# A graph-attention and mean-aggregation kernel: a new setup order, an earlier score store and other first banks

## Chip, cores and metric

The kernel runs on one core of a Trainium2 chip (trn2). The metric is the device time of one execution in microseconds. The time before is the median of three runs, 3327.2 us.

## What is computed

Two layers for 16 graphs of 1024 nodes with 512 features. The first is attention over neighbours with 8 heads of 64 units; the second averages the neighbours' rows, joins them to the own row and multiplies by a weight. Each has a relu, a residual and a layer norm.

```python
feats   = einsum('bnf,hfu->bhnu', x, W)
e_self  = einsum('bhnu,hu->bhn', feats, a_self)
e_neigh = einsum('bhnu,hu->bhn', feats, a_neigh)
dense   = leaky_relu(e_self[..., :, None] + e_neigh[..., None, :], 0.2)
dense   = dense + NEG_BIG * (1.0 - A[:, None])
gat     = relu(concat_heads(einsum('bhij,bhju->bhiu', softmax(dense), feats) + b))
x1      = layernorm(x + gat)
agg     = einsum('bij,bjf->bif', adj, x1) / max(sum(adj, -1), 1e-6)
out     = layernorm(x1 + relu(einsum('bnf,of->bno', concat(x1, agg), W1)))
```

## The kernel before

The program is written by hand for five engines, each with its own list of instructions, joined by semaphores. SyncE issues all DMAs, in the order in which they are written. One graph is one batch. 1024 nodes are T = 8 row tiles of 128, and 512 features are KC = 4 chunks. TensorE has 8 banks of PSUM.

**A batch** (`batch` in each engine's list) has these stages. The features are products of transposed rows with layer one's weights, each operand split in a high and a low part, so one feature tile is 12 matmuls of 512 columns (`features`, `split_product`, recorded at line 889 as all matmuls are). The scores of all 16 score rows come from 12 matmuls for each half of the nodes (`scores`) with weights that were multiplied by the attention vectors beforehand. ScalarE copies each half into sc_row (`score_rows`, line 486). SyncE stores the row to memory (`store_scores`, line 345) and loads each head's row back, broadcast over the partitions, into s_bc (`load_scores`, line 350). In the heads, ScalarE makes a step word for each of 64 pairs of head and key tile (`make_step`, line 497) from s_bc, VectorE shifts it by the adjacency into a mask word (`mask_word`, line 727), and TensorE multiplies 8 query tiles by 3 parts and 2 kinds for each (`key_tile`, 48 matmuls of 65 columns). VectorE also makes the values of each head (`value_parts`, lines 631 to 637) and adds up the sums (`head_sums`, lines 653 and 655). After the heads come the layer norm (VectorE, ScalarE and GpSimd), the aggregation with the transposed adjacency (`aggregate`, 128x512 matmuls), and layer two (`own`, `neighbours`).

**Overlap of batches.** The rows of the next batch are transposed (`turn_x`, line 918), copied (`x_high`, line 462) and split (`x_low`, line 664) inside the batch; its first half of scores and its feature tiles 0 to 3 stand between the heads and the aggregation. Feature tiles 0 and 1 are computed into banks 0 and 1, tiles 2 and 3 into banks 4 and 5; VectorE empties them with the bias (`feature_rows`, line 669). The aggregation uses the banks AGG_BANKS, (0, 1, 2, 6) for the first half and (7, 3, 0, 1) for the second, and TensorE waits for ft_sb 2 of the next batch before its first matmul, which goes to bank 0.

**Around a batch's end.** SyncE transposes the adjacency words of the next batch (`turn_adj`, line 327), stores output tiles (`store_y`, line 340), and ends the batch with the store of tile 7. Then `first_scores` stores the second score half of the next batch, waits until both halves have landed, and loads the rows of heads 0 and 1. y_out and the slots 2 and 3 of the mask words are the same memory; VectorE waits for the y stores before it makes the values of head 0 (lines 709 and 710), and for the transposes before mask word 0.

**The setup, before batch 0.** SyncE loads layer one's weights, the first four row tiles, the attention vectors, the bias, layer two's weights (2 MB, into the memory xs of the layer's input), row tiles 4 to 7 and adjacency tiles 2 and 3. It then waits for all of layer two's transposes, loads the eight x tiles into xs, and the other adjacency tiles. VectorE splits layer one's weights (lines 600 and 602), makes the attention weights in 16 passes of 512 elements (lines 608 and 610) and splits them. TensorE waits for layer two's weights, turns them in eight groups through banks 0 and 1 (line 898), ScalarE copying (line 467) and VectorE splitting (line 620), and then for the attention weights. Only then come row tiles 0 to 3, `scores(0, 0)`, four feature tiles and row tiles 4 to 7. ScalarE makes the eight adjacency words (`adj_words`, line 480) last, and each word from the fourth on waits for a transpose to free one of three slots.

Of the kernel before, what the change touches and what calls it, by code (L numbers as in the profile page):

```python
# [15 lines left out]
P = 128  # L16
# [27 lines left out]
def gat_sage_kernel(nc, x, adj, gat_w, gat_b, gat_self, gat_neigh, sage_w, out):  # L44
# [22 lines left out]

    XT_BANKS = (6, 7, 6, 7, 0, 1, 0, 1)
# [6 lines left out]
    with ExitStack() as ctx:  # L75
# [106 lines left out]
        def adj_rows_at(t):  # L182
# [5 lines left out]
        w_raw = feat[:, 0:4, :, :].rearrange("p a b c -> p (a b c)")[:, 0:KC * HU].rearrange(  # L188
            "p (c n) -> p c n", c=KC)
        a_bc = z  # L190
        prod = y_out
# [106 lines left out]
        def _(sp):  # L298
            for c in range(KC):
                sp.dma_start(w_raw[:, c, :].rearrange("p (h u) -> p h u", h=H),  # L300
                             gat_w[:, col(c), :].rearrange("h p u -> p h u")).then_inc(w_in[0], 16)
            for t in range(HALF):
                sp.dma_start(lead_x[:, t, :], x[0, t * P:(t + 1) * P, :]).then_inc(lead_in[t].sem, 16)
# [3 lines left out]
            sp.dma_start(sage_raw, sage_w.rearrange("(c p) f -> p c f", p=P)).then_inc(w_in[3], 16)  # L307
# [5 lines left out]

            def load_lead(b, t):
                sp.dma_start(lead_x[:, t, :], x[b, t * P:(t + 1) * P, :]).then_inc(lead_in[t].sem, 16)
# [36 lines left out]
            def first_scores(b):  # L352

                store_scores(b, 1)
                sp.wait_ge(s_stored.sem, s_stored.at(b, 32))
                load_scores(b, 0)
                load_scores(b, 1)
# [5 lines left out]
            sp.wait_ge(w1_ps, 2 * KC)  # L363
            for t in range(T):
                load_x(0, t)
# [3 lines left out]
            store_scores(0, 0)  # L369
            for t in range(T):  # L370
                turn_adj(0, t)
                if t + 4 < T:
                    load_adj(0, t + 4)
            for b in range(B - 1):
                first_scores(b)
                for s in range(2):
                    sp.wait_ge(deg_row.sem, deg_row.at(b, 5 + s))
                    load_lead(b + 1, 2 * s)
                    load_lead(b + 1, 2 * s + 1)
# [30 lines left out]
                store_y(b, T - 1)  # L410
# [49 lines left out]
        def _(act):  # L460
# [4 lines left out]
            for c in range(2 * KC):  # L465
                act.wait_ge(w1_ps, c + 1)
                copy(w1h[:, c, :], bank[c % 2][:]).then_inc(w1_hi, 1)
# [117 lines left out]
            for t in range(HALF):  # L585
                x_high(0, t)
            score_rows(0, 0)
# [3 lines left out]
            for t in range(T):  # L591
                adj_words(0, t)
# [4 lines left out]
        def _(dve):  # L597
# [5 lines left out]
            dve.wait_ge(w_in[1], 32)  # L603
            dve.wait_ge(consts, N_CONST)
            n = 0
            for c in range(KC):
                for k in range(2):
                    dve.tensor_tensor(prod[:, 0], w_raw[:, c, :], a_bc[:, k, :], ALU.mult).then_inc(wa_step, 1)
                    dve.wait_ge(wa_step, n + 1)
                    dve.tensor_reduce(wa32[:, c, k * H:(k + 1) * H], prod[:, 0].rearrange("p (h u) -> p h u", h=H),  # L610
                                      AX.X, ALU.add).then_inc(wa_step, 1)
                    dve.wait_ge(wa_step, n + 2)
                    n += 2
            dve.tensor_copy(wah, wa32[:]).then_inc(w_ready, 1)
            dve.wait_ge(w_ready, 3)
            dve.tensor_tensor(wal, wa32[:], wah.bitcast(F32),
                              ALU.subtract).then_inc(w_ready, 1)
            for c in range(2 * KC):
                dve.wait_ge(w1_hi, c + 1)
                dve.tensor_tensor(w1l[:, c, :], bank[c % 2][:], w1h[:, c, :].bitcast(F32),  # L620
                                  ALU.subtract).then_inc(w1_lo, 1)
# [57 lines left out]
            def batch(b, more):  # L679
# [29 lines left out]
                for s in range(2):  # L709
                    dve.wait_ge(y_stored[s], b * (16 * T // 2) + 16)  # L710
# [22 lines left out]
                feature_rows(b, 7)  # L733
                mask_word(2)
# [138 lines left out]

            dve.wait_ge(w_in[2], 16)
            ones_column(0)
            for t in range(HALF):
                x_low(0, t)
            for t in range(HALF):
                feature_rows(0, t)
            first_maximum(0)  # L880
            for t in range(HALF, T):
                x_low(0, t)
            for b in range(B):
# [3 lines left out]
        def _(pe):  # L887
# [4 lines left out]
            pe.wait_ge(consts, 1)  # L892
            pe.wait_ge(w_in[3], 16)
            for f in range(2 * KC):
                if f >= 2:
                    pe.wait_ge(w1_lo, f - 1)
                for c in range(KC):
                    ins = pe.transpose(bank[f % 2][:, col(c)], sage_raw[:, c, f * P:(f + 1) * P], ident[:])
                ins.then_inc(w1_ps, 1)
            pe.wait_ge(w1_lo, 2 * KC)  # L900
            pe.wait_ge(w_ready, 4)
            pe.wait_ge(consts, N_CONST)
# [37 lines left out]
            def batch(b, more):  # L940
# [60 lines left out]
                if more:  # L1001
# [7 lines left out]
                    pe.wait_ge(ft_sb.sem, ft_sb.at(b + 1, 2))  # L1009
# [34 lines left out]
                def aggregate_first(jt, part):  # L1044
                    part_ok = (x1_hi, x1_lo)[part]
                    pe.wait_ge(part_ok.sem, part_ok.at(b, jt + 1))
                    for f in range(KC):
# [26 lines left out]

            for t in range(HALF):
                turn_x(0, t)
            scores(0, 0)
            for t in range(HALF):
                features(0, t)
            pe.wait_ge(ft_sb.sem, ft_sb.at(0, 2))  # L1080
            for t in range(HALF, T):
                turn_x(0, t)
            for b in range(B):
# [23 lines left out]
```

## Time and profile before

| | us |
|---|---|
| runs (three), median | 3327.2 (3321.91 to 3328.36) |
| profiled execution, its own time | 3327.12 |
| span of its one core | 3325.3 |
| TensorE busy | 3233.3 |
| VectorE busy | 2353.1 |
| ScalarE busy | 1866.8 |
| GpSimd busy | 283.5 |

The profile is one execution. The span is divided among the engines as busy time, and idle time before an instruction is put down to whatever released it. The ends of matmuls are modelled, so the pitch from one start to the next tells their real cost. In a timeline a bracket shows the idle time before a row and its releaser.

### The profile page before, as it was taken

How to read it: one execution, taken by the hardware profiler on the slowest of the kernel's cores; microseconds unless marked ns; L12 is line 12 of the kernel's file. 1: busy time of each engine (PE TensorE's matmuls, PEld its weight loads, DVE VectorE, ACT ScalarE, POOL GpSimd, SP SyncE). 2: the span in 40 equal slices, each digit the busy share in tenths (PEclk: the TensorE clock that was granted, in tenths of full speed). 3: DMA queues.
4: the chain of work that ended last, by engine and by line, in shares of the span. 5: the costliest groups of instructions: out<-in, count | busy, mean ns of one | idle time of the engine just before them, and what ended most of it. 6: DMA issues, size and time to landing. Idle time of an engine off the chain costs nothing.

```text
span 3325.3 us, 124497 instructions
## 1 busy us (share of the span) xinstructions
PE 3233.3 (97%) x56896; PEld 2747.0 (83%) x56896; DVE 2353.1 (71%) x4236; ACT 1866.8 (56%) x2456; POOL 283.5 (9%) x251
## 2 busy tenths in 40 slices
PE   4999999999999999999999999999999999999998
PEld 3978879788796978969789697897978879697895
DVE  3857858587685867858678585785858758587685
ACT  2746647365564655646466474664746647465563
POOL 0020100202002020010200102010020200202001
PEclk8999999999999999999999999999999999999999
DMA  6235251341514315252162422525135151441501
GB/s 180 73 64 149 62 138 55 92 128 57 143 61 105 108 50 151 67 111 89 50 157 67 113 88 59 150 64 131 64 79 140 57 143 50 105 119 51 135 32 51
DMA packets 368653, 314.48 MB, mean 95 GB/s; under 512 B 285056, under 2 KB 285056, under 8 KB 368128
## 3 DMA queue, kind: packets, MB, share of 16 engines
q1 hardware_dynamic: 368128, 306.52, 34.1%
q8 instruction: 446, 7.31, 0.9%
q14 instruction: 79, 0.65, 0.1%
HBM read 205.26 MB, written 34.08 MB: 72 GB/s over the span
## 4 chain that ended last, share of the span: by engine, by line
PE 84%; DVE 7%; DMA 5%; ACT 2%; issue 1%; SPq 0%; DVEq 0%; POOL 0%; ACTq 0%
PE six L889 73%; PE pair L889 10%; DVE mask L727 2%; DMA s_bc<-self_scores 2%; DMA out_dram<-mask 1%; DMA self_scores<-sc_row 1%; PE pair L918 1%; DVE rest L635 1%; PE six L918 1%; DVE x_parts L631 1%; ACT trh L462 1%; DVE feat L669 1%; ACT step L497 1%; DMA adj_t<-adj_word 0%; DVE trl L664 0%
## 5 line engine op out<-in xcount | busy, mean ns | idle before, releaser
L889 PE MATMUL six<-x_parts,mask 128*128 128x65 bf16 x16384 | 1547.9, 192 | 21.1 <-DVE mask L727 21.1
L889 PEld LDWEIGHTS six<-x_parts,mask 128*128 128x128 fp8e4 x16384 | 1536.8, 97 | 30.2 <-issue 20.5
L889 PE MATMUL six<-third,mask 128*128 128x65 bf16 x16384 | 1547.7, 192 | 1.9 <-issue 1.6
L889 PE MATMUL six<-rest,mask 128*128 128x65 bf16 x16384 | 1548.0, 195 | 1.3 <-issue 1.2
L889 PEld LDWEIGHTS six<-third,mask 128*128 128x128 fp8e4 x16384 | 1537.0, 98 | 2.5 <-issue 2.4
L889 PEld LDWEIGHTS six<-rest,mask 128*128 128x128 fp8e4 x16384 | 1531.7, 96 | 1.7 <-issue 0.8
L497 ACT ACTIVATE step<-s_bc,n_step 128x1024 uint16<-128x1024 f32 x1024 | 1089.1, 1137 | 378.3 <-DVE mask L727 344.7
L727 DVE TENSOR_TENSOR mask<-adj_t,step 128x1024 uint16<-128x1024 uint16 x1024 | 649.9, 685 | 60.5 <-ACT step L497 60.5
L889 PE MATMUL six<-adj_t,x_parts 128*128 128x512 fp8e4 x1536 | 385.2, 379 | 16.2 <-DVE trl L857 5.4
L440 POOL TENSOR_TENSOR s_bc<-feat,rden 128x512 f32<-128x512 f32 x112 | 124.6, 1118 | 2789.9 <-DVE s_bc L770 2776.2
L889 PEld LDWEIGHTS six<-adj_t,x_parts 128*128 128x128 f16 x1536 | 144.8, 98 | 206.1 <-issue 19.6
L462 ACT ACTIVATE mask<-six,rdeg 128x512 f32<-128x512 f32 x128 | 87.9, 687 | 234.8 <-PE six L889 234.8
L653 DVE TENSOR_TENSOR x_parts<-six,qry_w 128x130 f32<-128x130 f32 (+2 forms) x272 | 110.6, 407 | 145.4 <-PE six L889 145.1
L889 PE MATMUL six<-w1h,trh 128*128 128x512 f32 x512 | 210.0, 410 | 0.0
L462 ACT ACTIVATE trh<-six 128x512 fp32r<-128x512 f32 x160 | 87.9, 598 | 203.3 <-PE six L889 171.3
L889 PE MATMUL six<-w1l,trh 128*128 128x512 f32 x512 | 199.7, 390 | 0.0
L889 PE MATMUL six<-w1h,trl 128*128 128x512 f32 x512 | 199.7, 390 | 0.0
L857 DVE TENSOR_TENSOR trl<-six,trh 128x512 fp32r<-128x512 f32 x96 | 60.2, 683 | 186.1 <-ACT trh L462 186.1
L520 ACT ACTIVATE x_parts<-xs,nb,rs 128x512 f16<-128x512 f32 x128 | 104.2, 814 | 141.4 <-DVE nb L791 141.4
L889 PE MATMUL six<-w0h,trh 128*128 128x512 f32 x448 | 177.1, 395 | 0.0
L889 PE MATMUL six<-w0l,trh 128*128 128x512 f32 x448 | 177.1, 395 | 0.0
L446 POOL TENSOR_TENSOR x_parts<-xs,x_parts 128x512 f16<-128x512 f32 x128 | 160.8, 1256 | 190.5 <-ACT xs L523 190.5
(125 smaller groups left out, 4566.9 us busy)
## 6 DMA issues: line engine op xcount, KB each, us to landing
s_bc<-self_scores SPq DMA_DIRECT2D x128, 512.0 KB, 3.8
mask<-in_adj_dram SPq DMA_DIRECT2D x64, 512.0 KB, 4.5
xs<-in_x_dram SPq DMA_DIRECT2D x128, 256.0 KB, 4.2
adj_nat<-in_adj_dram SPq DMA_DIRECT2D x64, 512.0 KB, 4.3
out_dram<-mask SPq DMA_DIRECT2D x128, 256.0 KB, 3.5
adj_nat<-in_x_dram SPq DMA_DIRECT2D x64, 256.0 KB, 5.8
step<-in_x_dram SPq DMA_DIRECT2D x64, 256.0 KB, 3.9
xs<-in_L_gnn_W_dram SPq DMA_DIRECT2D x1, 2048.0 KB, 12.3
```

The costliest lines, as they stand in the source:

```text
L440: pool.tensor_tensor(z[:, t % 2].rearrange("p (h u) -> p h u", h=H), feat[:, t, :, 0:U], rden[:, t, :].unsqueeze(2).broadcast_to([P, H, U] ...
L446: pool.tensor_tensor(x1l[:, t, :], xs[:, t, :], x1h[:, t, :], ALU.subtract).then_inc(x1_lo.sem, 1)
L462: return act.activation(o, i, ACT.Copy, scale=scale)
L497: act.activation(step[:, g % STEP_SLOTS], s_bc[:, h % 2], ACT.Sigmoid, scale=STEP, bias=n_step[:, jt, h:h + 1]).then_inc(stepped.sem, 1)
L520: act.activation(x1h[:, t, :], xs[:, t, :], ACT.Identity, bias=nb[:, t:t + 1], scale=rs[:, t:t + 1]).then_inc(x1_hi.sem, 1)
L631: dve.tensor_tensor(whole, feat[:, tiles, h, :].unsqueeze(1).broadcast_to([P, 2, n, U1]), key_w[:, :, tiles, h:h + 1].to_broadcast([P, 2, ...
L635: dve.tensor_tensor(rest, whole, first, ALU.subtract).then_inc(val_rest.sem, 1)
L653: dve.tensor_tensor(scaled, sums[:, :, :, 1, :], factor, ALU.mult).then_inc(lower_ok.sem, k1 - k0)
L727: dve.tensor_tensor(mask[:, g % MASK_SLOTS], adj_t[:, jt, :], step[:, g % STEP_SLOTS], ALU.logical_shift_left).then_inc(masked.sem, 1)
L857: dve.tensor_tensor(trl[:, f, :], bank[AGG_BANKS[half][f]][:], trh[:, f, :].bitcast(F32), ALU.subtract).then_inc(aggt_lo.sem, 1)
L889: return pe.matmul(o, l, r, start=start, stop=stop, skip_group_check=True)
L918: ins = pe.transpose(bank[XT_BANKS[t]][:, col(k)], source[:, col(k)], ident[:])
```

## The change

The setup is put in another order, and so are three places of a batch. In the setup, row tile 0 is loaded first; the attention weights are made in four passes of 2048 elements from memory of their own (x1_parts, which is free at that time), after the first four row tiles are split; TensorE turns row tiles 0 to 3, makes their features, then the scores, row tiles 4 to 7, and last layer two's weights, through banks 2 and 3. Layer two's weights are loaded after the adjacency tiles 0 and 1; the x tiles are loaded after the first score rows of batch 0. ScalarE makes adjacency words 0 to 3 after the first four row tiles and words 4 to 7 between the copies of layer two's last four groups. In a batch, the scores' store is ahead of the last output store of the batch before; VectorE waits for the y stores before mask word 2; and the aggregation's first part opens with banks 2, 6, 7 and 3 before it waits for ft_sb 2 and goes to banks 0 and 1.

```diff
+    W1_BANKS = (2, 3)
-        w_raw = feat[:, 0:4, :, :].rearrange("p a b c -> p (a b c)")[:, 0:KC * HU].rearrange(
-            "p (c n) -> p c n", c=KC)
+        w_raw, prod = (pool32[:, i * KC * HU:(i + 1) * KC * HU].rearrange("p (c n) -> p c n", c=KC) for i in range(2))
-        prod = y_out
@@ sync
+            load_lead(0, 0)
             for c in range(KC):
                 sp.dma_start(w_raw[:, c, :].rearrange("p (h u) -> p h u", h=H),
                              gat_w[:, col(c), :].rearrange("h p u -> p h u")).then_inc(w_in[0], 16)
-            for t in range(HALF):
-                sp.dma_start(lead_x[:, t, :], x[0, t * P:(t + 1) * P, :]).then_inc(lead_in[t].sem, 16)
+            for t in range(1, HALF):
+                load_lead(0, t)
...
-            sp.dma_start(sage_raw, sage_w.rearrange("(c p) f -> p c f", p=P)).then_inc(w_in[3], 16)
...
                 store_scores(b, 1)
+                if b >= 1:
+                    store_y(b - 1, T - 1)
...
-            sp.wait_ge(w1_ps, 2 * KC)
-            for t in range(T):
-                load_x(0, t)
             for s in range(2):
                 sp.wait_ge(xt_ps.sem, xt_ps.at(0, 2 * s + 2))
                 load_adj(0, s)
-            store_scores(0, 0)
+            sp.dma_start(sage_raw, sage_w.rearrange("(c p) f -> p c f", p=P)).then_inc(w_in[3], 16)
             for t in range(T):
                 turn_adj(0, t)
                 if t + 4 < T:
                     load_adj(0, t + 4)
+                if t == HALF - 1:
+                    store_scores(0, 0)
             for b in range(B - 1):
                 first_scores(b)
+                if b == 0:
+                    sp.wait_ge(w1_ps, 2 * KC)
+                    for t in range(T):
+                        load_x(0, t)
...
                 turn_adj(b + 1, T - 1)
-                store_y(b, T - 1)
@@ scalar
             for t in range(HALF):
                 x_high(0, t)
+            for t in range(4):
+                adj_words(0, t)
             score_rows(0, 0)
             act.wait_ge(ft_ps.sem, ft_ps.at(0, HALF))
             for t in range(HALF, T):
                 x_high(0, t)
-            for t in range(T):
-                adj_words(0, t)
+            for t in range(2 * KC):
+                w1_high(t)
+                if t >= KC:
+                    adj_words(0, t)
@@ vector
+            def attention_weights():
+                dve.wait_ge(w_in[1], 32)
+                dve.wait_ge(consts, N_CONST)
                 for k in range(2):
-                    dve.tensor_tensor(prod[:, 0], w_raw[:, c, :], a_bc[:, k, :], ALU.mult).then_inc(wa_step, 1)
-                    dve.wait_ge(wa_step, n + 1)
-                    dve.tensor_reduce(wa32[:, c, k * H:(k + 1) * H], prod[:, 0].rearrange("p (h u) -> p h u", h=H),
+                    if k:
+                        dve.wait_ge(wa_step, 2)
+                    dve.tensor_tensor(prod, w_raw, a_bc[:, k, :].unsqueeze(1).broadcast_to([P, KC, HU]),
+                                      ALU.mult).then_inc(wa_step, 1)
+                    dve.wait_ge(wa_step, 2 * k + 1)
+                    dve.tensor_reduce(wa32[:, :, k * H:(k + 1) * H], prod.rearrange("p c (h u) -> p c h u", h=H),
                                       AX.X, ALU.add).then_inc(wa_step, 1)
...
                 feature_rows(b, 5)
-                for s in range(2):
-                    dve.wait_ge(y_stored[s], b * (16 * T // 2) + 16)
...
                 feature_rows(b, 7)
+                for s in range(2):
+                    dve.wait_ge(y_stored[s], b * (16 * T // 2) + 16)
                 mask_word(2)
...
+            for t in range(HALF):
+                x_low(0, t)
+            attention_weights()
             dve.wait_ge(w_in[2], 16)
             ones_column(0)
             for t in range(HALF):
-                x_low(0, t)
-            for t in range(HALF):
                 feature_rows(0, t)
-            first_maximum(0)
             for t in range(HALF, T):
                 x_low(0, t)
+            first_maximum(0)
+            for c in range(2 * KC):
+                w1_low(c)
@@ tensor
-                    pe.wait_ge(ft_sb.sem, ft_sb.at(b + 1, 2))
...
+                    if jt == 0 and part == 0:
+                        for half, f in ((0, 2), (0, 3), (1, 0), (1, 1)):
+                            aggregate(half, f, jt, part)
+                        if more:
+                            pe.wait_ge(ft_sb.sem, ft_sb.at(b + 1, 2))
+                        aggregate(0, 0, jt, part)
+                        aggregate(0, 1, jt, part)
+                        return
...
+            pe.wait_ge(consts, N_CONST)
             for t in range(HALF):
                 turn_x(0, t)
-            scores(0, 0)
+            pe.wait_ge(w_ready, 2)
             for t in range(HALF):
                 features(0, t)
+            pe.wait_ge(w_ready, 4)
+            scores(0, 0)
             pe.wait_ge(ft_sb.sem, ft_sb.at(0, 2))
             for t in range(HALF, T):
                 turn_x(0, t)
+            pe.wait_ge(w_in[3], 16)
+            for f in range(2 * KC):
+                turn_w1(f)
+            pe.wait_ge(w1_lo, 2 * KC)
```

## Rows read from the trace of the kernel before

**Rows 1.** The page, busy time, share of the span, instructions of TensorE

```profile
PE 3233.3 (97%) x56896; PEld 2747.0 (83%) x56896; DVE 2353.1 (71%) x4236; ACT 1866.8 (56%) x2456; POOL 283.5 (9%) x251
```

**Rows 2.** Waits of TensorE: us in total, times, longest

```profile
PE six L889 <- DVE mask L727: 21.1, 28, 3.2
PE six L898 <- DMA xs<-in_L_gnn_W_dram: 20.1, 1, 20.1
PE six L889 <- issue: 9.0, 22, 0.7
```

**Rows 3.** Timeline of TensorE, setup: start, duration, instruction, idle before

```profile
25.81 1.97 PE L898 MATMUL six<-ident,xs 128*128 128x128 f32 x8 [3.81 <-DVE w1l L620]
...
33.53 1.97 PE L918 MATMUL pair<-ident,adj_nat 128*128 128x128 f32 x8 [1.41 <-DVE w1l L620]
...
40.10 0.63 PE L889 MATMUL pair<-trl,wah_wide 128*128 128x512 f32 x1
...
42.66 0.63 PE L889 MATMUL pair<-trl,wah_wide 128*128 128x512 f32 x1
...
44.10 0.39 PE L889 MATMUL six<-w0h,trh 128*128 128x512 f32 x1
...
55.01 0.39 PE L889 MATMUL six<-w0h,trl 128*128 128x512 f32 x1
...
77.36 1.03 PE L954 MATMUL six<-ident,sc_row 16*128 16x16 f32 x8 [11.49 <-ACT sc_row L462]
...
88.54 0.21 PE L889 MATMUL six<-x_parts,mask 128*128 128x65 bf16 x1
```

**Rows 4.** Timeline of VectorE, setup: the split of layer one's weights

```profile
8.68 2.29 DVE L602 TENSOR_TENSOR w0l<-feat,w0h 128x2048 fp32r<-128x2048 f32 x1
```

**Rows 5.** Tile s_bc, setup: duration ns min/median/max, first and last start

```profile
L608 DVE TENSOR_TENSOR mask<-feat,s_bc x8: 691/692/693, 13.1 to 23.2; 128x512 f32<-128x512 f32 x8
```

**Rows 6.** Timeline of ScalarE, setup: the last adjacency word

```profile
75.68 1.06 ACT L480 ACTIVATE adj_word<-mask 128x1024 uint16<-128x1024 f32 x1 [1.11 <-DMA adj_t<-adj_word]
```

**Rows 7.** DMA issues of the first 100 us: size, median us to landing

```profile
xs<-in_L_gnn_W_dram SPq DMA_DIRECT2D x1, 2048.0 KB, 12.3
```

**Rows 8.** The chain that ended last, first boundary: start, us, what

```profile
282.91 0.33 SPq L340
...
283.28 2.32 DMA self_scores<-sc_row
...
285.62 3.94 DMA s_bc<-self_scores
...
290.86 0.69 DVE mask L727
```

**Rows 9.** Timeline of ScalarE, first and last of 15 boundaries

```profile
281.50 0.59 ACT L462 ACTIVATE sc_row<-six 16x512 f32<-16x512 f32 x1 [1.65 <-PE six L889]
...
3129.53 0.59 ACT L462 ACTIVATE sc_row<-six 16x512 f32<-16x512 f32 x1 [1.65 <-PE six L889]
```

**Rows 10.** Timeline of SyncE's queue, first and last of 15 boundaries

```profile
280.56 1.45 SPq L327 DMA_TRANSPOSE adj_t<-adj_word  x1
...
3131.08 0.33 SPq L345 DMA_DIRECT2D self_scores<-sc_row  x1
```

**Rows 11.** Tile self_scores, whole span: landing of the broadcast loads

```profile
DMA to landing us min/median/max: 3.3/3.8/6.8
```

**Rows 12.** Timeline of TensorE, opening of the first aggregation

```profile
201.27 0.39 PE L889 MATMUL six<-w0h,trl 128*128 128x512 f32 x1
202.09 0.81 PE L889 MATMUL six<-adj_t,x_parts 128*128 128x512 fp8e4 x3 [0.43 <-issue]
```

**Rows 13.** Timeline of VectorE, the same place

```profile
201.31 0.68 DVE L669 TENSOR_TENSOR feat<-six,bias_bc 128x512 f32<-128x512 f32 x1
```

**Rows 14.** Tile adj_word, setup: landing of the adjacency transposes

```profile
DMA to landing us min/median/max: 2.8/4.7/5.9
```

**Rows 15.** Window of 4 us in the setup: busy by engine, granted clock, DMA share, GB/s

```profile
36.00:40.00 4.00, 2.44 (x9) 1.93 (x10) 2.08 (x4) 1.33 (x3) 0.00 (x0) 0.50 1.01 341
```

More of the change, by code:

```diff
@@ L298, in _, with load_lead @@
         def _(sp):
+            def load_lead(b, t):
+                sp.dma_start(lead_x[:, t, :], x[b, t * P:(t + 1) * P, :]).then_inc(lead_in[t].sem, 16)
+            load_lead(0, 0)
             for c in range(KC):
@@ L312, in load_x @@
                 sp.dma_start(xs[:, t, :], x[b, t * P:(t + 1) * P, :]).then_inc(x_in[t].sem, 16)
-            def load_lead(b, t):
-                sp.dma_start(lead_x[:, t, :], x[b, t * P:(t + 1) * P, :]).then_inc(lead_in[t].sem, 16)
             def load_tail(b, t):
@@ L462, in copy, with w1_high @@
                 return act.activation(o, i, ACT.Copy, scale=scale)
-            for c in range(2 * KC):
+            def w1_high(c):
                 act.wait_ge(w1_ps, c + 1)
-                copy(w1h[:, c, :], bank[c % 2][:]).then_inc(w1_hi, 1)
+                copy(w1h[:, c, :], bank[W1_BANKS[c % 2]][:]).then_inc(w1_hi, 1)
             def x_high(b, t):
@@ L602, in _, with w1_low @@
             dve.tensor_tensor(w0l[:], w_raw, w0h[:].bitcast(F32), ALU.subtract).then_inc(w_ready, 1)
[L603 to L606, printed above, removed]
+            def attention_weights():
+                dve.wait_ge(w_in[1], 32)
+                dve.wait_ge(consts, N_CONST)
                 for k in range(2):
-                    dve.tensor_tensor(prod[:, 0], w_raw[:, c, :], a_bc[:, k, :], ALU.mult).then_inc(wa_step, 1)
-                    dve.wait_ge(wa_step, n + 1)
-                    dve.tensor_reduce(wa32[:, c, k * H:(k + 1) * H], prod[:, 0].rearrange("p (h u) -> p h u", h=H),
-                                      AX.X, ALU.add).then_inc(wa_step, 1)
[L612 to L618, printed above, removed]
+                    if k:
[4 more added lines that the diff above has]
+                    dve.tensor_reduce(wa32[:, :, k * H:(k + 1) * H], prod.rearrange("p c (h u) -> p c h u", h=H),
+                                      AX.X, ALU.add).then_inc(wa_step, 1)
+                dve.wait_ge(wa_step, 4)
+                dve.tensor_copy(wah, wa32[:]).then_inc(w_ready, 1)
+                dve.wait_ge(w_ready, 3)
+                dve.tensor_tensor(wal, wa32[:], wah.bitcast(F32),
+                                  ALU.subtract).then_inc(w_ready, 1)
+            def w1_low(c):
                 dve.wait_ge(w1_hi, c + 1)
-                dve.tensor_tensor(w1l[:, c, :], bank[c % 2][:], w1h[:, c, :].bitcast(F32),
+                dve.tensor_tensor(w1l[:, c, :], bank[W1_BANKS[c % 2]][:], w1h[:, c, :].bitcast(F32),
                                   ALU.subtract).then_inc(w1_lo, 1)
@@ L889, in mm, with turn_w1 @@
                 return pe.matmul(o, l, r, start=start, stop=stop, skip_group_check=True)
-            pe.wait_ge(consts, 1)
-            pe.wait_ge(w_in[3], 16)
-            for f in range(2 * KC):
+            def turn_w1(f):
                 if f >= 2:
@@ L897, in _ @@
                 for c in range(KC):
-                    ins = pe.transpose(bank[f % 2][:, col(c)], sage_raw[:, c, f * P:(f + 1) * P], ident[:])
+                    ins = pe.transpose(bank[W1_BANKS[f % 2]][:, col(c)], sage_raw[:, c, f * P:(f + 1) * P], ident[:])
                 ins.then_inc(w1_ps, 1)
-            pe.wait_ge(w1_lo, 2 * KC)
-            pe.wait_ge(w_ready, 4)
-            pe.wait_ge(consts, N_CONST)
             def split_product(o, lh, ll, rh, rl, first=True, last=True):
```

## Prediction

> **What bounds the kernel now.** I read the busy times first. TensorE is busy for 97% of the span [rows 1], so an edit pays only where it shortens TensorE's work or one of its waits. The change removes no matmul from a batch. The second view is therefore the list of TensorE's waits [rows 2]: 20.1 us for layer two's weights at the start, 21.1 us in 28 pieces for VectorE's masks, and 9.0 us in 22 pieces that are put down to issue. The third step was to find the place of each.
>
> The first lies in the setup. TensorE's timeline [rows 3] shows another of 11.5 us there, for the second score row (77.36), and has the first head matmul at 88.54 us; from there to the end it is nearly always at work. Everything earlier is setup, 88.5 us, with far less matmul work in it. The mask waits lie at the start of the heads: 15 times, once for each batch after the first, TensorE waits for mask 0, and mostly once more for mask 7, which ends a VectorE chain that starts with mask 0. The windows around the 15 boundaries hold 0.5 to 3.2 us each. The issue pieces lie for the most part at the opening of the aggregation.
>
> The profiled execution took 3327.1 us around its span of 3325.3 us; the median of the runs shown is 3327.2 us, so sums against the profile need no correction. About 0.2% (7 us) is what a measurement of this kernel can tell from no change.
>
> **Part 1, the setup.** I replay the new order with durations of the old rows. The queue of SyncE has one row-tile load ahead of the layer-one weights, about 0.5 us more before VectorE can split them. Splitting ended at 10.97 us [rows 4], now about 11.5. The first four row tiles are then transposed, copied and split through two banks. TensorE is through with them at about 14.5 us, and starts the 48 matmuls of the first four feature tiles. Their pitch at the start of such a burst is 0.427 us (40.10 to 42.66, six steps) for about nine matmuls, and 0.232 us after it (44.10 to 55.01, 47 steps) [rows 3]: 9 x 0.427 + 39 x 0.232 = 12.9 us, to 27.3 us.
>
> Beside it VectorE makes the attention weights. Before, this was 16 passes of 512 elements a partition, 0.69 us each at a pitch of 0.72, from 13.1 to 24.7 us, ahead of everything [rows 5]. A reduction of 2048 elements has no row; above it are four small ones, 2.8 us, below it half of that, 1.4 us, if it ran at twice their rate. The multiplication has the weights' subtraction as its neighbour, the same shape, 2.29 us [rows 4]. I take 2.29 us for all four, since both kinds took 0.69 us in the small form, and 0.5 us for two small splits: 15.9 + 9.2 + 0.5 = 25.6 us. That is under 27.3 us, so the pass costs nothing while the features cover it; without that cover it would cost 9.7 us. The Trainium skill, "VectorE: DVE Perf Modes", section on the TRN2 errata, says that operands in SBUF cost a fixed latency once an instruction, so that large tiles pay it once; by that the four passes would save some 12 such starts, which the cover makes worthless either way.
>
> The 12 score matmuls follow: 2.8 us, to 30.1 us. Row tiles 4 to 7 are turned, through ScalarE and VectorE, in one cycle of two banks (2.56 us, see below) and one turn more, about 3.3 us, to 33.4 us. Then come layer two's weights, eight groups through two banks. The old rhythm is 2.56 us a pair (25.81 to 33.53, three pairs) [rows 3]: four pairs are 10.2 us. ScalarE now makes an adjacency word between the copies of the last groups, 1.06 us each [rows 6]; three of them count, with one partly hidden: 2.9 us. So the weights are done at 46.5 us. Their 2 MB load is issued behind the adjacency loads at about 14.5 us, and had a landing time of 12.3 us before [rows 7]; it is needed only at 33.4, so the 20.1 us wait is gone. The eight adjacency transposes cost TensorE 11.5 us before, because nothing was left to run beside them and score row two stood behind the last word on ScalarE. Now four go under the features and four under the weights. The eight loads of layer one's input are moved behind the first score loads; SyncE issues them in some 3.5 us and their first reader is VectorE's residual after the heads, a hundred microseconds later.
>
> After the weights TensorE has 24 matmuls to the second score row, nine at the slow pitch: 3.8 + 3.5 = 7.3 us, to 53.8. 36 more at 0.232 us (8.4 us) and the small groups (1.0 us, as at 77.36) bring it to the heads at 63.3 us. The mask's side: copy 0.6, to 54.4, then as in the chain of a boundary 2.3 for the store, 3.9 for the load, 1.3 to the mask's start and 0.7 for the mask [rows 8]: 62.7 us. TensorE is last, barely. Gain: 88.5 - 63.3 = **25.2 us**. Bounds: 19 us if the weights take the slow pitch at every turn and the words are not hidden, 29 us if the clock comes up early.
>
> **Part 2, scores stored first.** In the chain of the first boundary [rows 8] the store of the last output tile goes out at 282.9, the scores' store at 283.28, lands at 285.60, the broadcast load lands at 289.56, and mask 0 starts at 290.86. But the score row was ready at 282.09 [rows 9], and SyncE had issued its transpose by 282.01 [rows 10]. The scores' store waited for a y tile that VectorE finished late. With the new order it goes at 282.1, 1.2 us earlier; at the last boundary the same difference is 1.0 us (3130.12 against 3131.08) [rows 9, 10], and the 15 lie between 0.9 and 1.6 us. The y store then goes when its tile is ready, as before: SyncE is free again 0.4 us after the scores' store, and its next wait is 2 us long. VectorE's wait for that store moves to mask 2, some 9 us after its issue. In that order mask 0 and all of its chain come 1.2 us earlier; a boundary can give back no more than it has. The lesser of the two, summed over 15 boundaries, is 16 us of the 21.1 us. What takes some of it: the loads now overlap the y store for 1.2 us more. A broadcast load took 3.3 to 6.8 us [rows 11]. I take **15.5 us**; bounds 6 us (0.65 us of each advance lost in the load) and 20 us (all stalls go, the store lands earlier with no y data ahead of it).
>
> **Part 3, aggregation in free banks.** The last feature matmul starts at 201.27, the first aggregation at 202.09 instead of 201.50, as VectorE's second feature tile ends only at 201.99 [rows 12, 13]. Four matmuls of the aggregation (three take from 202.09 to 202.73, 0.21 us each) into banks 2, 6, 7 and 3 now fill that time. The idle shown is 0.43 us, the pitch says 0.59. Twelve of 15 openings look like this, three have half: 5.2 us by the one, 7.7 by the other. I take **6 us**, bounds 0 and 8. Later waits in the aggregation don't take it back: the x parts are a tile or more ahead. The last batch has no such opening.
>
> Sum: 25.2 + 15.5 + 6 = 46.7 us; 3327.1 - 46.7 = **3280.4 us**.
>
> **The rivals.** (a) Transposes behind the 2 MB load. The first adjacency transpose is now issued with the weights' load ahead of it, and word 3, score row one and the copies of tiles 4 to 7 stand behind it on ScalarE. If the load lands 12.3 us after 14.5 and the transpose 2.8 to 5.9 us after that [rows 7, 14], word 3 ends at 31 to 34 us, the tiles start 1 to 4 us late: 3284 us at the worst. For it: SyncE's queue issues both. Against: the features run to 30 us anyway. The Trainium skill, "DMA: Bandwidth & Descriptors", section on queues, rings and completion order, says that a DMA's semaphore lands only after every earlier write of that DMA engine; by that this is what would happen, since the rows cannot show the two together. Chance 0.15.
>
> (b) The setup runs at the lower clock. Between 36 and 40 us, after much idling, the granted clock was 0.50, the 1.2 GHz level, and the matmuls that followed had the slow pitch [rows 3, 15]. If it stays there for all 120 matmuls up to the heads instead of 18, that is 102 x 0.195 = 20 us more: 3300 us. Against: both bursts of before rose after about nine. The Trainium skill, "TensorE: Matmul & The Clock Gate", section on what is actually happening, has the clock fall with idling and rise with sustained work; the rows agree. Chance 0.05.
>
> (c) The boundary gives nothing, since load and y store share the DMA engines and the load lands when it did: 3296 us. For: the 256 KB of the y store now stand between the scores' store and the loads. Against: they stood ahead of both before. Chance 0.1.
>
> (d) Slower: the same overlap makes the load late. Setup and opening give 31 us; to lose that and 7 us more, each boundary must lose 2.5 us net, so the load must take 3.9 + 1.2 + 2.5 = 7.6 us at each. At 8.0 us the time is 3340 us. Not one load of 128 took over 6.8 us [rows 11]. Chance 0.03.
>
> (e) The order changes and the time doesn't, the stalls coming back as waits for VectorE in the heads: within 7 us, 3324 us. Chance 0.03.
>
> My forecast has 0.64. Faster: 0.64 + 0.15 + 0.05 + 0.1 = 0.94; same 0.03; slower 0.03. The range: all bounds good give 3270, setup 19, boundaries 8 and opening 3 give 3297, which takes in (a) and (c).
>
> **What would show it.** The first head matmul at 61 to 66 us; no TensorE wait for the weights' load, and none of 11 us for a score row. The scores' store ahead of the last y store at each boundary, mask waits down from 21 us to 3 to 9 us. Aggregation 0.23 us after the last feature matmul. Heads starting after 75 us, or mask waits above 15 us, would prove me wrong.

## The result, and the profile after

The changed kernel took 3281.9 us (median of four runs, 3279.8 to 3285.1) against 3327.0 us before: 45.1 us less, a ratio of 0.9872 with a 95% interval of 0.9860 to 0.9884. The prediction was 3280.4 us. The profiled execution took 3279.8 us around a span of 3278.0 us, 47.3 us less than the old span.

The page and the waits of TensorE after the change (columns as in [rows 1] and [rows 2]):

```profile
PE 3228.9 (99%) x56896; PEld 2745.0 (84%) x56896; DVE 2351.1 (72%) x4224; ACT 1866.4 (57%) x2456; POOL 284.0 (9%) x251
```

```profile
PE pair L925 <- DMA adj_nat<-in_x_dram: 7.6, 2, 4.0
PE six L901 <- DVE mask L734: 7.6, 17, 0.6
...
PE six L901 <- issue: 4.3, 10, 1.0
...
PE six L901 <- DVE w1l L629: 2.4, 1, 2.4
```

The wait of 20.1 us for layer two's weights is gone, and so is that of 11.5 us for the second score row; two waits for the first row tiles, 7.6 us in all, stand at the start. The 21.1 us for masks are 7.6, and the 9.0 us of issue (time for which the profile shows no releaser) are 4.3. TensorE's timeline of the setup shows the rest:

```profile
11.98 1.94 PE L925 MATMUL pair<-ident,adj_nat 128*128 128x128 f32 x8 [2.15 <-DVE trl L673]
13.57 0.78 PE L901 MATMUL six<-w0h,trh 128*128 128x512 f32 x1
...
25.85 0.40 PE L901 MATMUL pair<-trh,wah_wide 128*128 128x512 f32 x1
...
32.89 1.90 PE L908 MATMUL six<-ident,xs 128*128 128x128 f32 x8
...
45.54 0.79 PE L901 MATMUL six<-w0h,trh 128*128 128x512 f32 x1 [2.39 <-DVE w1l L629]
...
62.90 0.20 PE L901 MATMUL six<-x_parts,mask 128*128 128x65 bf16 x1
```

The features begin at 13.6 us, the scores at 25.9, layer two's weights at 32.9 and are done at 45.5, and the heads begin at 62.9 us where they began at 88.5 [rows 3]. VectorE's four large passes run beside the features; the first two, from its timeline:

```profile
15.19 2.28 DVE L616 TENSOR_TENSOR x_parts<-x_parts,s_bc 128x2048 f32<-128x2048 f32 x1
17.51 2.29 DVE L619 TENSOR_REDUCE wa<-x_parts 128x32 f32<-128x2048 f32 x1
```

At the first boundary, the first step of the kernel before stood here in ScalarE's timeline:

```profile
289.58 7.39 ACT L497 ACTIVATE step<-s_bc,n_step 128x1024 uint16<-128x1024 f32 x7 [1.92 <-DMA s_bc<-self_scores]
```

The chain of the changed kernel stands against this, [rows 8] and [rows 9] (start, us, what):

```profile
255.82 0.60 ACT sc_row L465
256.42 0.02 issue
256.44 2.74 DMA self_scores<-sc_row
259.18 0.02 issue
259.20 4.14 DMA s_bc<-self_scores
263.34 0.02 issue
263.36 1.16 ACT step L500
```

The scores' store now goes out as soon as the row is there. But from the row's end to the first step it was 7.49 us before (282.09 to 289.58) and it is 6.94 us now (256.42 to 263.36): 0.55 us is gained of the 1.2 us by which the store moved. The store itself takes 2.74 us to land, where it took 2.32. Over the 15 boundaries, the median from the row's end to the first step went from 7.56 to 6.97 us.

The opening of the aggregation, TensorE's timeline, against [rows 12]:

```profile
176.16 0.39 PE L901 MATMUL six<-w0h,trl 128*128 128x512 f32 x1
176.39 0.39 PE L901 MATMUL six<-adj_t,x_parts 128*128 128x512 fp8e4 x1
```

The first aggregation matmul follows the last feature matmul at 0.23 us instead of 0.82.

### The profile page after: what moved, and what is told of

It is laid out like the page before. It is cut to its first block, busy times and chain, and to the rows that moved or that the text cites. A ratio compares the mean times of both kernels' runs of the same rounds, so it can differ in the third digit from the quotient of the medians.

```text
span 3278.0 us, 124485 instructions
## 1 busy us (share of the span) xinstructions
PE 3228.9 (99%) x56896; PEld 2745.0 (84%) x56896; DVE 2351.1 (72%) x4224; ACT 1866.4 (57%) x2456; POOL 284.0 (9%) x251
## 4 chain that ended last, share of the span: by engine, by line
PE 90%; DVE 5%; DMA 3%; ACT 1%; issue 1%; SPq 0%; DVEq 0%; POOL 0%; ACTq 0%
PE six L901 78%; PE pair L901 10%; DVE mask L734 2%; DMA s_bc<-self_scores 1%; DMA self_scores<-sc_row 1%; PE pair L925 1%; PE six L925 1%; DVE rest L644 1%; DVE x_parts L640 1%; ACT step L500 0%; DVE trl L866 0%; ACT trh L465 0%; DMA adj_nat<-in_adj_dram 0%; DVE feat L678 0%; DVE third L646 0%
## 5 line engine op out<-in xcount | busy, mean ns | idle before, releaser
L901 PEld LDWEIGHTS six<-x_parts,mask 128*128 128x128 fp8e4 x16384 | 1536.0, 97 | 16.5 <-issue 8.2
```

The costliest lines, as they stand in the source:

```text
L901: return pe.matmul(o, l, r, start=start, stop=stop, skip_group_check=True)
```

## The experiments

All runs were timed against the kernel before on the same chip, in three groups. The kernel before was at 3325.9, 3324.0 and 3324.3 us in them. The changed kernel, run once more in the third, was at 3281.6 us, so differences of 2 us between medians are not to be read as effects. It was not run in the first two, and "above the changed kernel" means there above its 3281.9 us of the section before.

**The three parts, undone one by one.** First the opening:

```diff
                     pe.wait_ge(sc_f32.sem, sc_f32.at(b + 1, 1))
+                    pe.wait_ge(ft_sb.sem, ft_sb.at(b + 1, 2))
...
-                    if jt == 0 and part == 0:
-                        for half, f in ((0, 2), (0, 3), (1, 0), (1, 1)):
...
```

> The changed kernel (3281.9 us) with the old opening of the aggregation alone: TensorE waits for the second feature tile before its first aggregation matmul. Theory 1, the pitch counts: 12 openings lose 0.56 us, three some 0.3: 7.7 us, 3289.6 us. Theory 2, the idle shown counts (0.41 us each): 5.2 us, 3287.1 us. Rival, the lost time is absorbed by later slack: 3282 us.

Measured: 3288.7 us, ratio 0.9891 (0.9878 to 0.9905), 6.8 us above the changed kernel. This lies between the two theories and excludes neither; the rival of no effect is below all four runs (3288.2 to 3292.1). TensorE's issue waits were 9.8 us here and 4.3 in the changed kernel.

Then the order of the stores:

```diff
                 store_scores(b, 1)
-                if b >= 1:
-                    store_y(b - 1, T - 1)
...
                 turn_adj(b + 1, T - 1)
+                store_y(b, T - 1)
...
                 feature_rows(b, 5)
+                for s in range(2):
+                    dve.wait_ge(y_stored[s], b * (16 * T // 2) + 16)
...
                 feature_rows(b, 7)
-                for s in range(2):
-                    dve.wait_ge(y_stored[s], b * (16 * T // 2) + 16)
```

> The changed kernel with the old order of the scores' store and the last y store, and the old place of VectorE's wait for the y stores. Theory 1, what the two traces show (mask waits at the 15 boundaries 21.2 us before, 6.6 after): 14.6 us lost, 3296.5 us. Theory 2, a typical boundary has its first step only 0.55 us earlier after the change and the rest of the difference is chance in one profile (one wait of 3.2 us, two of 1.8): 8 to 9 us lost, 3290.5 us. Rival, nothing at the boundaries: 3282 us.

Measured: 3291.1 us, ratio 0.9894 (0.9879 to 0.9909), 9.2 us above. TensorE's waits in this kernel:

```profile
PE six L900 <- DVE mask L735: 16.5, 27, 1.2
```

So with the old order this run had 16.5 us of mask waits, not 21.1: the long wait of 3.2 us of the old profile did not come again. Theory 2 fits better, and the 13.5 us by which the two first profiles differ is partly chance. (The 6.6 us in the expectation are too low: in the changed kernel's trace all 7.6 us lie at the 15 boundaries, and batch 0's waits are put down to issue.)

> The kernel before with the new setup alone (opening and store order as before). Theory: the first head matmul comes 25.6 us earlier as in the changed kernel, less about 1 us of a mask wait in batch 0: 3302 us. If the setup's gain is partly given back in the batches, it is above 3305 us; if the batches gave more than the traces suggest, under 3298 us. With the two runs above, the three parts should add up to 45 us within 3 us.

This kernel is the changed one with both edits above. Measured: 3301.1 us, ratio 0.9924 (0.9912 to 0.9937), 24.8 us under the kernel before. Its mask waits were 19.1 us in 26 pieces, the longest 2.1 us.

Undone one at a time, the three parts are 24.8, 9.2 and 6.8 us, 40.8 us in all against 44 to 45 for the whole. But each of the last two can also be read from this kernel, which has neither. Adding the store order alone gives the kernel of the first run: 3301.1 - 3288.7 = 12.4 us. Adding the opening alone gives that of the second: 3301.1 - 3291.1 = 10.0 us. So the store order is worth 9.2 us with the new opening in place and 12.4 without it, the opening 6.8 or 10.0; the two together are 19.2 us either way. Whether the 3.2 us between the two readings are an interaction or the scatter of four medians was not settled: runs of one kernel spread over 3.4 to 5.8 us here.

**What holds the scores' store.** Two kernels change what is around it in SyncE's queue.

```diff
                 if b >= 1:
-                    store_y(b - 1, T - 1)
+                    sp.wait_ge(y_ok.sem, y_ok.at(b - 1, T))
                 sp.wait_ge(s_stored.sem, s_stored.at(b, 32))
                 load_scores(b, 0)
                 load_scores(b, 1)
+                if b >= 1:
+                    store_y(b - 1, T - 1)
```

> The changed kernel with the last y store issued behind the two broadcast loads of the scores (its tile is still waited for at the old place). Question: after the change the scores' store lands 2.8 us after its issue, before it was 2.3 us, so half of the 1.2 us advance is lost. Theory A, the 256 KB y store that follows it slows it and the loads: the store lands in 2.3 us or less, mask waits fall from 7.6 to under 3 us, 3276 us. Theory B, what is ahead in the queue (the adjacency transpose issued 1.5 us before) holds it: landing stays at 2.8 us, time 3282 us within 2 us.

Measured: 3289.6 us, ratio 0.9893 (0.9879 to 0.9906): 7.7 us slower than the changed kernel. Its chain at the first boundary:

```profile
255.52 2.94 DMA self_scores<-sc_row
...
258.53 4.68 DMA s_bc<-self_scores
```

The y store is no longer near the scores' store, and that lands no earlier. Theory A is out. B's landing is right and its time is not: I had not expected the loads to suffer. The first took 4.7 us against 4.1, and TensorE's mask waits are 14.5 us. It is so at all 15 boundaries: from the issue of the loads to the first step there are 4.3 to 4.8 us, where the changed kernel has 3.8 to 4.4. The kernels' difference is only that the y store is behind the two loads instead of 0.8 us behind the scores' store.

```diff
                 store_scores(b, 1)
                 if b >= 1:
+                    turn_adj(b, T - 1)
                     store_y(b - 1, T - 1)
...
-                turn_adj(b + 1, T - 1)
```

> The changed kernel with the last adjacency transpose of the next batch issued behind the scores' store instead of 1.5 to 2 us ahead of it. Theory B, the transpose ahead holds the store's landing: the store lands in 2.3 us or less instead of 2.8 to 3.0 us; the loads now have the transpose ahead of them and take more than 4.1 us. Theory C, 2.8 us is simply what a small store takes when the ring has been quiet: landing unchanged. For the time both leave it open (the transpose only changes its place in the queue): 3278 to 3288 us.

Measured: 3286.1 us, ratio 0.9883 (0.9868 to 0.9898). The chain at the first boundary no longer contains the store's landing at all; it goes through SyncE's queue:

```profile
256.69 0.30 SPq L344
...
257.04 1.24 SPq L326
...
258.33 0.59 SPq L339
...
258.96 4.79 DMA s_bc<-self_scores
```

The store had landed by the time the queue came to the loads, 2.27 us after its issue, at all 15 boundaries; in the changed kernel it took 2.7 to 3.2 us in most. That fits theory B and excludes C. One row of the changed kernel supports it without any edit, in SyncE's timeline of batch 0, where no transpose and no store stands close ahead:

```profile
54.04 0.28 SPq L344 DMA_DIRECT2D self_scores<-sc_row  x1
55.51 0.82 SPq L349 DMA_DIRECT2D s_bc<-self_scores  x2
```

Here the store lands within 1.5 us. B is not the whole account, though: at two of the 15 boundaries of the changed kernel (660 and 2681 us) the store was issued right behind the transpose as well and landed in 2.1 us. Why was not looked into. The loads behind the transpose took 4.8 us, so moving the transpose gives nothing: the store no longer stands behind it, and the loads do.

**The setup's cover.**

```diff
             for t in range(2 * KC):
                 w1_high(t)
-                if t >= KC:
-                    adj_words(0, t)
+            for t in range(HALF, T):
+                adj_words(0, t)
```

> The changed kernel with adjacency words 4 to 7 made by ScalarE after all eight copies of layer two's weights, not between them. Theory: in the changed kernel a word stands ahead of the copy on ScalarE three times, so layer two's weights are split at 45.5 us; without it they are at 43 to 43.5 us, the words end at about 49 us, paced by the transposes, before the second score row is ready, and the first head matmul comes at 60.5 to 61.5 us instead of 62.9: 1.5 to 2.5 us faster, 3280 us. Rival, the words then delay the second score row on ScalarE and the heads come later than 62.9 us.

Measured: 3279.6 us, ratio 0.9864 (0.9849 to 0.9878). TensorE's timeline and two windows of it (columns as in [rows 15]), then the same windows of the changed kernel:

```profile
44.67 0.50 PE L901 MATMUL six<-w0h,trh 128*128 128x512 f32 x1 [1.41 <-DVE w1l L629]
...
59.98 0.20 PE L901 MATMUL six<-x_parts,mask 128*128 128x65 bf16 x1
```

```profile
44.00:48.00 4.00, 3.33 (x14) 2.74 (x15) 0.61 (x1) 3.18 (x7) 0.00 (x0) 1.00 0.43 97
48.00:52.00 4.00, 4.00 (x20) 3.02 (x19) 0.81 (x2) 1.56 (x3) 0.00 (x0) 1.00 0.75 168
```

```profile
44.00:48.00 4.00, 2.46 (x6) 1.97 (x7) 0.69 (x1) 1.80 (x5) 0.00 (x0) 0.50 0.86 195
48.00:52.00 4.00, 4.00 (x15) 3.16 (x14) 0.00 (x0) 0.00 (x0) 0.00 (x0) 0.76 0.00 1
```

The heads come 2.9 us earlier, but only 0.9 us of that is the weights (45.54 to 44.67), less than the theory's 2. The other 2 us are the clock: between 44 and 48 us, where the features of row tiles 4 to 7 begin, the granted clock was 1.00 (2.4 GHz), and 0.50 (1.2 GHz) in the changed kernel, which had ten matmuls at the slow pitch there. In the kernel with both edits further down the same order met a clock of 0.55, and its heads began at 61.0 us. The gain in the weights is near 1 us. The 2 us of the clock can't be booked for the edit, since the second kernel with it did not have them; and the time alone, 2 us under the changed kernel, is not clear of the scatter.

```diff
-            sp.dma_start(sage_raw, ...).then_inc(w_in[3], 16)
             for t in range(T):
                 turn_adj(0, t)
+                if t == 0:
+                    sp.dma_start(sage_raw, ...).then_inc(w_in[3], 16)
```

> The changed kernel with layer two's 2 MB load issued behind the first adjacency transpose instead of ahead of it. Theory, rival (a) of the prediction: the first transpose (issued 22.65 us, landed 28.77 us, 6.1 us) is held by the 2 MB load; without it, it lands in 3 to 4 us, word 3 is done by 28 us, score row one is copied at 28.8 us instead of 29.9 us, and turning row tiles 6 and 7 starts about 1 us earlier. The load then lands at 33 to 36 us instead of 27.7 us, so TensorE waits for it up to 2 us: net between 1 us faster and 2 us slower. If the first transpose still takes 6 us, the load was not what held it.

Measured: 3281.2 us, ratio 0.9868 (0.9852 to 0.9885): no change in time. The chain of the changed kernel, and ScalarE's timeline of the changed kernel and of this one:

```profile
22.65 6.12 DMA adj_t<-adj_word
```

```profile
28.85 1.06 ACT L483 ACTIVATE adj_word<-mask 128x1024 uint16<-128x1024 f32 x1 [3.95 <-DMA adj_t<-adj_word]
...
29.91 0.57 ACT L465 ACTIVATE sc_row<-pair 16x512 f32<-16x512 f32 x1
```

```profile
26.40 1.06 ACT L484 ACTIVATE adj_word<-mask 128x1024 uint16<-128x1024 f32 x1 [0.67 <-DMA adj_t<-adj_word]
...
30.43 0.59 ACT L466 ACTIVATE sc_row<-pair 16x512 f32<-16x512 f32 x1 [2.88 <-PE pair L902]
```

The first transpose landed 6.1 us after its issue with the 2 MB load ahead of it, and word 3 waited 3.95 us; with the load behind it the wait is 0.67 us. The mechanism of rival (a) is there: in the changed kernel word 3 ended at 29.9 us and the score row's copy came right behind it, though TensorE's scores had ended about 1 us before. With the edit the copy waits for TensorE instead. It comes no earlier in this run because the scores themselves were late: they began at 27.4 us where the changed kernel's began at 25.9, as the row tiles had landed later and more matmuls had the slow pitch. The same edit in the last kernel of this section met an ordinary start and had the copy at 28.5 us, 1.4 us earlier. So the price of (a) is about 1 us at this place, too little for the time to show.

```diff
-                for k in range(2):
-                    dve.tensor_tensor(prod, w_raw, a_bc[:, k, :]...broadcast_to([P, KC, HU]), ...)
+                for c in range(KC):
+                    for k in range(2):
+                        dve.tensor_tensor(prod[:, 0], w_raw[:, c, :], a_bc[:, k, :], ...)
```

> The changed kernel with the attention weights made by the old 16 passes of 512 elements in the new place. The new four passes ran from 15.2 to 24.4 us and the scores began at 25.85 us, so there are 1.0 us of cover. 16 passes at a pitch of 0.72 us take 11.6 us and end 2.3 us later. Theory, the cover is used up: TensorE waits about 1.3 us for them, and VectorE reaches the first feature tiles 2.3 us later; the first head matmul comes 1 to 2.3 us later than 62.9 us. Rival, word 3 on ScalarE (ready at 29.9 us) is the later wait anyway and hides it: no change of the heads' start.

Measured: 3282.6 us, ratio 0.9876 (0.9862 to 0.9891). TensorE's timeline:

```profile
27.66 0.50 PE L902 MATMUL pair<-trh,wah_wide 128*128 128x512 f32 x1 [1.32 <-DVE wal_wide L625]
```

The wait is there, 1.32 us as worked out, and the heads began at 63.1 us against 62.9. The score row was copied at 30.99 us, right behind word 3, so word 3 was the later wait, as the rival has it. There is a reserve: in eight profiles with the changed setup, the heads began between 61.6 and 62.9 us, so 1 us more or less cannot be read from one. The four large passes take 9.3 us where the 16 small ones take 11.6, and that is worth nothing that shows here. What made them free was their new place, under the features.

**What is left at a boundary.** The last four runs look at the wait for mask 7.

> The changed kernel once more, on the chip of the next three runs, as their base. 3282 us within 2 us; mask waits of TensorE 7 to 10 us in all, mostly one of 0.5 to 0.6 us a boundary at mask 7.

Measured: 3281.6 us (3279.7 to 3283.1), mask waits 8.8 us in 22 pieces of at most 0.6 us.

```diff
-                    if jt == (4 if h else 6) and h < H - 1:
+                    if jt == (4 if h else 7) and h < H - 1:
                         value_parts(b, h + 1)
```

> The changed kernel with VectorE's three passes for the values of head 1 behind mask 7 instead of behind mask 6. Theory: what is left at a boundary (0.5 to 0.6 us, and 1.0 us in batch 0) is TensorE's wait for mask 7, which stands behind 3.7 us of value passes; with mask 7 ahead of them the wait is gone, the values still end at the same moment, about 0.8 us before TensorE needs them, and mask 8 follows 0.2 us before its need: mask waits from 8 us to under 3 us, 5 to 6 us faster, 3276 us. Rival, the wait only moves to the values or mask 8 of head 1: 3282 us, waits for the values (third) or mask 8 in place of mask 7.

Measured: 3275.4 us (3273.7 to 3276.5), ratio 0.9851 (0.9838 to 0.9865): 6.2 us faster than the run above, with no overlap of their runs. TensorE's waits:

```profile
PE six L901 <- DVE mask L734: 4.4, 13, 0.5
```

The mask waits were halved, not removed. At the first boundary there is none left. Batch 0 keeps 0.7 us, put down to issue. Five boundaries still wait 0.2 to 0.4 us for mask 0, 1.6 us in all. The other eight pieces, 2.8 us, are new: one lies 30 us and seven lie 55 us after the score row, in later heads, where the changed kernel and its second run have none. In the one shown, VectorE had just made the values of another head (710.6 to 714.4 us):

```profile
715.08 0.20 PE L901 MATMUL six<-x_parts,mask 128*128 128x65 bf16 x1 [0.49 <-DVE mask L734]
```

So theory and rival both have a part: the waits left at a boundary are down to 1.6 us of 8.8, and 2.8 us have come back in later heads.

> The changed kernel with the adjacency words 4 to 7 last in the setup (2 to 3 us) and the values of head 1 behind mask 7 (5 to 6 us). If both hold and add: 3274 us. If the masks' part is not there: 3279 us.

Measured: 3276.3 us, ratio 0.9854 (0.9841 to 0.9868). The two do not add up to anything that can be told from the values' edit alone.

> As the run with both, and layer two's load behind the first adjacency transpose. With words last the chain of the setup goes word 3, score row one, tiles 4 to 7, weights; word 3 comes 2 us earlier, which moves the tiles by up to 1.1 us: 3273 us, heads at 59 us. Rival, the load lands too late (34 us): TensorE waits for it and the heads start no earlier than with both.

Measured: 3273.9 us (3272.5 to 3277.7), ratio 0.9848 (0.9835 to 0.9862), heads at 59.0 us. It is the fastest median, 50.3 us under the kernel before and 7.7 us under the changed kernel of its group; against the values' edit alone its runs overlap, so only that edit is shown to pay. Of its rival a part was there: TensorE waited 0.82 us for layer two's load, but the heads came 2 us earlier than with both edits all the same.

## Why the prediction was right, and where it was not

The time was right within 1.5 us. The three terms of the sum can now be told apart, and part of that closeness is luck: the boundaries were put too high and the opening, by both readings, too low. Together they were to give 21.5 us and gave 19.2.

**Setup, 25.2 us predicted, 24.8 us measured** (the kernel with the setup alone); the heads began at 62.9 us against a predicted 63.3. Its steps were right in order and mostly in size: features at 13.6 against 14.5, four passes of 2.28 and 2.29 us against 2.29, weights done at 45.5 against 46.5, TensorE last at the heads by little (mask 0 starts at 60.8 us and the heads at 62.9). Small errors cancel. The features began 0.9 us early and had five slow matmuls instead of nine; the row tiles 4 to 7 took 4.3 us instead of 3.3, as the copy of the score row stood behind word 3; the weights took 12.7 instead of 13.1; and from there to the heads there were 17.4 us instead of 16.8, with ten slow matmuls instead of nine. The passes cost nothing, as said, but the small ones cost nothing that shows either; the price of 9.7 us without cover was not tested. (The sums of this part are off by 0.1 us in a few places, which changes nothing: 14.5 and 12.9 make 27.4, and 46.5, 7.3, 8.4 and 1.0 make 63.2.)

**Boundaries, 15.5 us predicted, 9.2 us measured with the new opening and 12.4 without it.** This is the term that was mis-sized. The order of the stores moved the scores' store 1.2 us forward as predicted, and I let mask 0 follow by the whole of it. At a typical boundary it followed by 0.6 us, because the store's landing grew from 2.3 to mostly 2.7 to 3.2 us. Nothing in the old rows contradicts that: [rows 10] show the transpose issued right ahead, and [rows 8] the landing of a store that was issued 1.3 us after that transpose's issue had ended. I took 2.32 us for the price of a small store. The 1.5 us of batch 0 and the run with the transpose behind suggest that part of it was waiting for what was ahead.

What a boundary gave back can be read from one number. In the traces before and after, TensorE waits for mask 0 by what the time from the row's end to the first step has above 6.93 us: 0.57 us at 7.49, 3.17 at 10.10, 0.32 at 7.24, and none is listed where the time is 7.05 us or less. At 14 boundaries of 15 this wait was there before, 13.1 of the 21.1 us; after, it is 1.2 us at five. The other 8.0 us, for mask 7, are still 6.4. The prediction also has a mask 0 wait at all 15; at 2725 us there was none.

The other part of the error is that the 21.1 us [rows 2] belong to one execution. Their 3.2 us are one boundary, where the broadcast load was late; the others have 0.5 to 1.8 us. The three profiles with the old order have 21.1, 16.5 and 19.1 us of mask waits, and six with the new one, counting the runs that leave the boundaries as they are, 7.6 to 10.8: means of 18.9 and 9.3, 9.6 us apart. The result lies between the lower bound of 6 us, with half of each advance lost, and the 15.5 us. What I named as the loss, loads late beside the y store, is not it: from the loads' issue to the first step the median was 4.09 us before and 4.03 after, and with the y store behind the loads the time was 7.7 us longer.

**Opening, 6 us predicted, 6.8 us measured with the new store order and 10.0 without it.** The figure between the idle shown and the pitch stood up in the first reading only. The first aggregation matmul came at the pitch of its neighbours, 0.23 us, which was the step foretold.

**The rivals.** (a) has its mechanism: the Trainium skill, "DMA: Bandwidth & Descriptors", section on queues, rings and completion order, has a DMA's semaphore wait for the earlier writes of its DMA engine. The 6.1 us of the first transpose behind the 2 MB load, against 2.9 us or less when the load is behind (23.49 to 26.40 us), agree, and so do 2.7 us against 1.5 for the same store. They do not tell that order from a mere sharing of the DMA engines, which would delay them too. The price, up to 4 us, was about 1. (b) did not come for the whole setup, though the clock was at 0.50 at 44 us in the changed kernel; its ten slow matmuls there cost 2 us, of which the sum had nine. (c) and (d) put the loss on the loads; of (c) a part happened, half of the advance gone, for another reason. (e) did not happen. Mask waits of 7.6 us lie in the foretold 3 to 9 us, but that one profile is the lowest of six, and three of them are above 9: the sign was met by a favourable execution.

## What to carry to other kernels

Moving a small transfer forward in a queue takes away what was put behind it; what still stands ahead of it can take part of that back, as the transpose did here. So the landing time of the old place is not the price of the new one.

Before a difference of two profiles is booked as a gain, undo the one edit: a single wait in the old profile was 3.2 us where its neighbours had 0.5 to 1.8. And undo it both with and without the other edits: here the two readings were 9.2 and 12.4 us.

Where an engine makes a batch of work just ahead of the item that the bottleneck waits for, exchange the two, and look for the wait further on: one number changed in VectorE's list was worth 6 us, as much as the edit of TensorE's opening, with 2.8 us of small waits new in a later head.

## What was not expected

A y store of 256 KB issued behind two loads of 512 KB makes the first of them land later (4.7 us against 4.1 at the first boundary, and 7.7 us in the time of 15 boundaries) than when it is issued 2 us ahead of them. Why a transfer behind another one in the same queue slows it more than one ahead was not settled.

TensorE's clock in the setup differs between profiles. Between 44 and 48 us the granted clock was 0.50 in all eight with the changed setup; in two with the words last, the same setup in both, it was 1.00 and 0.55. In the changed kernel it was 1.00 from 40 to 42 us, with TensorE busy for 0.8 us of the two, and at 0.50 by 44, after 0.7 us busy in the next two. The difference is worth 2 us at the start of the heads, so one profile can't price a setup edit of 1 us.

The granted clock of the record is also no guide at the very start: from 12 to 18 us it is shown as 1.00, while the features' first matmuls, at 13.6 to 15.8 us, have the slow pitch of 0.43 us.
